# Selective scans of two Mamba blocks: B products of three channel blocks through ScalarE and TensorE, C products of three on GpSimd

## The reference, cut to what matters

```python
delta = softplus(dt @ Wdt.T + dt_bias)
def step(state, xs):
    d_t, B_t, C_t, u_t = xs
    dA = jnp.exp(d_t[..., None] * A)
    state = dA * state + (d_t * u_t)[..., None] * B_t[:, None, :]
    y_t = jnp.einsum('bdn,bn->bd', state, C_t)
    return (state, y_t)
y = ys + u * D_param
y = y * silu(gate)          # layer 1 only
```

## Time and profile before

| what | before |
|---|---|
| time, median of 3 runs | 3902.34 us (3901.07 to 3902.68) |
| the profiled execution's own time | 3894.73 us |
| span of that execution in the trace | 3893.0 us |
| first scan stage with its opening | about 1085 to 1306 us |
| second and third, with openings | about 3337 to 3554, and 3555 to 3773 us |
| VectorE busy, whole span | 2307.4 us (59%) |
| ScalarE, GpSimd busy, whole span | 1531.7 us (39%), 1403.3 us (36%) |
| TensorE busy, whole span | 3553.1 us (91%) |
| mean granted TensorE clock | 0.963 |

### The profile page before, as it was taken

One profiled execution on the slowest core, in us unless ns is written; L12 is line 12 of the kernel. 1 busy time (PEld: TensorE's weight loads), 2 busy tenths in 40 slices (PEclk: granted clock), 3 DMA queues, 4 the chain that ended last, 5 costly groups with the idle time before them and its releaser, 6 DMA issues. The chain is left out here.

```text
span 3893.0 us, 74546 instructions
## 1 busy us (share of the span) xinstructions
PE 3553.1 (91%) x32040; PEld 2424.9 (62%) x32040; DVE 2307.4 (59%) x2562; ACT 1531.7 (39%) x2204; POOL 1403.3 (36%) x894
## 2 busy tenths in 40 slices
PE   6999999999768679999999999999999999686888
PEld 4556555555333455788888888888888847333334
DVE  4666666666369952555555555555555426698972
ACT  2555555555267421222222222222222103676740
POOL 3344444442079520122222222222222004597971
PEclk8999999999779889999999999999999999798999
DMA  6445555553122032011111111111111211221220
GB/s 207 127 138 149 139 139 148 142 137 92 39 92 92 20 141 87 25 43 36 49 41 49 41 49 41 47 43 41 49 41 45 78 52 37 80 92 60 92 66 22
DMA packets 229072, 302.22 MB, mean 78 GB/s; under 512 B 68592, under 2 KB 166864, under 8 KB 227456
## 3 DMA queue, kind: packets, MB, share of 16 engines
q1 hardware_dynamic: 228744, 297.45, 25.9%
HBM read 243.80 MB, written 53.13 MB: 76 GB/s over the span
## 5 line engine op out<-in xcount | busy, mean ns | idle before, releaser
L1764 POOL TENSOR_TENSOR D_ctx_lo<-D_ctx_raw,D_ctx_hi 128x2048 fp32r<-128x2048 f32 (+1 forms) x64 | 269.1, 4205 | 1218.6 <-ACT D_ctx_hi L1758 1218.6
L762 DVE TENSOR_REDUCE A_mxc<-A_psX 128x2 f32<-128x768 f32 (+2 forms) x512 | 485.4, 985 | 208.1 <-PE A_psX L792 207.2
L1058 ACT ACTIVATE A_probs<-A_psE 128x1024 f32<-128x1024 f32 (+1 forms) x416 | 426.2, 1025 | 318.0 <-PE A_psE L1091 312.9
L1783 ACT ACTIVATE D_V<-D_psY 128x384 f32<-128x384 f32 x208 | 101.9, 490 | 904.7 <-PE D_psY L1849 904.7
L1799 DVE TENSOR_REDUCE D_mxc<-D_psE 128x4 f32<-128x1536 f32 (+2 forms) x128 | 241.9, 1890 | 234.9 <-PE D_psE L1877 234.9
L2140 ACT ACTIVATE D_probs<-D_psE 128x2048 f32<-128x2048 f32 x112 | 210.5, 1879 | 296.0 <-PE D_psE L2253 296.0
L2269 PE MATMUL D_psO<-D_probs,D_V 128*32 128x256 f32 (+1 forms) x5376 | 313.3, 381 | 0.0
L1839 PE MATMUL D_psY<-D_ctx_hi,D_wk_hi 128*128 128x384 f32 (+2 forms) x768 | 279.8, 364 | 13.6 <-DVE D_K_lo L1794 12.7
L1849 PE MATMUL D_psY<-D_wv_hi,D_ctx_hi 128*128 128x384 f32 x832 | 285.6, 343 | 0.0
L1849 PE MATMUL D_psY<-D_wv_hi,D_ctx_lo 128*128 128x384 f32 x832 | 279.0, 335 | 0.0
L1849 PE MATMUL D_psY<-D_wv_lo,D_ctx_hi 128*128 128x384 f32 x832 | 278.7, 335 | 0.0
(11 more groups left out here) (376 smaller groups left out, 7797.5 us busy)
## 6 DMA issues: line engine op xcount, KB each, us to landing
A_land<-in_ctx SPq DMA_DIRECT2D x32, 768.0 KB, 6.0
D_ctx_raw<-in_ctx SPq DMA_DIRECT2D x32, 768.0 KB, 4.6
A_land<-in_ctx SPq DMA_DIRECT2D x16, 1024.0 KB, 5.7
D_ctx_raw<-in_ctx SPq DMA_DIRECT2D x16, 1024.0 KB, 5.3
E_Bn<-bc_scratch SPq DMA_DIRECT2D x64, 256.0 KB, 3.6
E_Cn<-bc_scratch SPq DMA_DIRECT2D x64, 256.0 KB, 3.4
k_scratch<-A_Khl SPq DMA_DIRECT2D x32, 384.0 KB, 5.4
A_Kst<-k_scratch SPq DMA_DIRECT2D x64, 192.0 KB, 3.6
```

Of the source, the lines that this page charges most:

```text
L762: nc.vector.tensor_reduce(mxc[:, u % 4, :, u // 4], psX[:, x % 2, :, 0:w], axis=AX_X, op=ALU.max).then_inc(x_free, 1)
L1058: nc.scalar.activation(probs[0:KW[k], n % NPR, :, :].rearrange("p h q -> p (h q)"), psE[0:KW[k], :], ACT.Exp, scale=HD ** -0.5).then_inc(e ...
L1764: nc.gpsimd.tensor_tensor(ctx_lo[c][:, :, 0:w], ctx_raw[c][:, :, 0:w], ctx_hi[c][:, :, 0:w].bitcast(F32), ALU.subtract).then_inc(lo_done[c ...
```

## The change

`B_ON_PE` becomes (0, 1, 2), so the entering terms of three blocks come through ScalarE and TensorE, and GpSimd makes only that of c = 3. `c_on_pool` becomes c > 0, so VectorE keeps only the C product of c = 0. The PSUM banks are now acc 4, h 1, dB 3, and all decays go to a ring of three SBUF buffers. The states that GpSimd reads (h_sb) are written over the part of du that is no longer needed; a row `B_du<-BS_dA,BS_dB` in the order below is such a scan. Rings change: dBx 4 to 2, hc 4 to 2, h_sb and hcp 3 to 4.

The openings change in three ways: the last du product is on VectorE instead of GpSimd, a one-column Exp is issued behind the Ln's, and the scan stage starts after four scaled copies instead of eight.

```diff
-B_ON_PE = (0, 2)
+B_ON_PE = (0, 1, 2)
 def c_on_pool(half, n, c):
-    return c in (1, 3) or c == 2 and n % 2 == 1
+    return c > 0
...
-        NS, NH, NP = 4, 4, 3
+        NS, NH, NP, ND, NE = 2, 2, 4, 3, 3
...
-        dA = r.ps("dA", [P, NA, HALF])
-        dA_sb = r.sb("dA_sb", [P, 2, HALF])
+        dA = r.sb("dA", [P, ND, HALF])
         h = r.ps("h", [P, HALF])
-        dB = r.ps("dB", [P, NB, HALF])
-        h_sb = r.sb("h_sb", [P, NP, HALF])
+        dB = r.ps("dB", [P, NE, HALF])
+        h_sb = du[:, 0:2, :].rearrange("p c (n t) -> p (c n) t", n=NP // 2)
...
         def decay(s):
-            return dA_sb[:, nth_pe[s] % 2, :] if s in nth_pe else dA[:, nth_b[s] % NA, :]
+            return dA[:, s % ND, :]
         def summed_at(s):
-            return s + (2 if s in nth_dve else 3)
+            return s + (2 if s in nth_dve else 4)
         def finished_at(s):
-            return s + (4 if STEPS[s][2] in B_ON_PE else 6)
+            return s + (4 if s in nth_dve else 7)
...
-                for m, i in pieces[:2 * TILES]:
+                for m, i in pieces[:TILES]:
                     times_b(m, i)
...
-                    if decay_ago(s) is not None:
-                        act.wait_ge(h_ready, decay_ago(s) + 1)
+                    if s >= ND:
+                        act.wait_ge(h_ready, s - ND + 1)
...
-                    for m, i in pieces[ahead:ahead + 1]:
+                    for m, i in pieces[ahead:ahead + (2 if s < TILES else 1)]:
...
-                multiplied = 0
-                for k, s in enumerate(b_on_pool):
-                    if k >= NS:
-                        while on_pool[multiplied] <= b_on_pool[k - NS]:
-                            times_c(on_pool[multiplied])
-                            multiplied += 1
+                for s in b_on_pool[:NS]:
                     times_b(s)
-                    half, n, c = STEPS[s]
-                    if gate is not None and half and n in (3, 6, 9, 12) and c == 1:
+                for s, (half, n, c) in enumerate(STEPS):
+                    if s in nth_pool:
+                        times_c(s)
+                    if s in nth_b and nth_b[s] + NS < len(b_on_pool):
+                        times_b(b_on_pool[nth_b[s] + NS])
+                    if gate is not None and half and n in (3, 6, 9, 12) and c == CN - 1:
                         gated_output(CN * (N_STATE - 1) + n // 3 - 1)
...
-                nc.vector.memset(dA[:, :, :], 0.0).then_inc(cleared, 1)
-                nc.vector.memset(dA_sb[:, :, :], 0.0).then_inc(cleared, 1)
+                nc.vector.memset(dA[:, :, :].rearrange("p k (b t) -> p k b t", t=S)[:, :, :, 0], 0.0
+                                 ).then_inc(cleared, 1)
...
-                for s in range(len(STEPS) + 3):
-                    if s in nth_pe and nth_pe[s] + NB < len(b_on_pe):
-                        entering(nth_pe[s] + NB)
+                for s in range(len(STEPS) + 4):
+                    if s in nth_pe and nth_pe[s] + NE < len(b_on_pe):
+                        entering(nth_pe[s] + NE)
...
-                        if c in B_ON_PE:
+                        if c in B_ON_PE or k == CN - 1:
                             dve.wait_ge(delta_made, k + 1)
                             nc.vector.tensor_tensor(du[:, c, :], delta[:, c, :], XnT[:, c, :], ALU.mult
                                                     ).then_inc(du_made, 1)
...
-                    for k, c in enumerate(ORDER):
+                    for k, c in enumerate(ORDER[:CN - 1]):
                         if c not in B_ON_PE:
                             pool.wait_ge(delta_made, k + 1)
...
+                    nc.scalar.activation(early[:, :], bias[:, 0:1], ACT.Exp)
```

More of the change, by code:

```diff
@@ L318, in _ @@
                 ahead = 0
-                for m, i in pieces[:2 * TILES]:
+                for m, i in pieces[:TILES]:
                     times_b(m, i)
                     ahead += 1
-                act.wait_ge(cleared, 2)
+                act.wait_ge(cleared, 1)
                 for s, (half, n, c) in enumerate(STEPS):
-                    if decay_ago(s) is not None:
-                        act.wait_ge(h_ready, decay_ago(s) + 1)
+                    if s >= ND:
+                        act.wait_ge(h_ready, s - ND + 1)
                     nc.scalar.activation(decay(s).rearrange("p (b t) -> p b t", t=S)[:, :, 1:S],
@@ L358, in times_c @@
                                             ALU.mult).then_inc(hcp_ready, 1)
-                multiplied = 0
-                for k, s in enumerate(b_on_pool):
-                    if k >= NS:
-                        while on_pool[multiplied] <= b_on_pool[k - NS]:
-                            times_c(on_pool[multiplied])
-                            multiplied += 1
-                    times_b(s)
-                    half, n, c = STEPS[s]
-                    if gate is not None and half and n in (3, 6, 9, 12) and c == 1:
+                for s in b_on_pool[:NS]:
+                    times_b(s)
+                for s, (half, n, c) in enumerate(STEPS):
[4 more added lines that the diff above has]
+                    if gate is not None and half and n in (3, 6, 9, 12) and c == CN - 1:
                         gated_output(CN * (N_STATE - 1) + n // 3 - 1)
-                for s in on_pool[multiplied:]:
-                    times_c(s)
             @block.vector
             def _(dve):
-                nc.vector.memset(dA[:, :, :], 0.0).then_inc(cleared, 1)
-                nc.vector.memset(dA_sb[:, :, :], 0.0).then_inc(cleared, 1)
+                nc.vector.memset(dA[:, :, :].rearrange("p k (b t) -> p k b t", t=S)[:, :, :, 0], 0.0
+                                 ).then_inc(cleared, 1)
                 def scan(s):
@@ L381, in scan @@
                         dve.wait_ge(db_full, nth_pe[s] + 1)
-                        entering = dB[:, nth_pe[s] % NB, :]
+                        entering = dB[:, nth_pe[s] % NE, :]
                     else:
@@ L435, in entering @@
                     pe.wait_ge(scaled_ready, TILES * (m + 1))
-                    if k >= NB:
-                        pe.wait_ge(h_ready, b_on_pe[k - NB] + 1)
+                    if k >= NE:
+                        pe.wait_ge(h_ready, b_on_pe[k - NE] + 1)
                     for i in range(TILES):
-                        last = nc.tensor.transpose(dB[:, k % NB, bass.ts(i, P)], scaled[:, m % 3, i, bass.ts(j, P)],
+                        last = nc.tensor.transpose(dB[:, k % NE, bass.ts(i, P)], scaled[:, m % 3, i, bass.ts(j, P)],
                                                    consts["ident"][:, :])
                     last.then_inc(db_full, 1)
-                for k in range(NB):
+                for k in range(NE):
                     entering(k)
@@ L1216, in l0_mamba @@
             q = Region(nc, inner, "B1")
+            early = q.sb("early", [P, 1])
             ps = q.ps("ps", [P, 8, 512])
@@ L2364, in l1_mamba @@
         ws = r.sb("ws", [P, DI], F32R)
-        duT = r.sb("duT", [P, NPAIR, len(B_ON_PE) * P])
         pr = r.sb("pr", [P, NPAIR, RN])
@@ L2376, in l1_mamba @@
             up = q.sb("up", [P, 2, B, PADDED])
-            eu = duT[:, :, :].rearrange("p t n -> p (t n)").rearrange("p (n t) -> p n t", n=2)
+            eu = q.sb("eu", [P, 2, TOK])
             wdt = q.sb("wdt", [P, DI])
@@ L2618, in l1_mamba @@
             q.restart()
+        duT = r.sb("duT", [P, NPAIR, len(B_ON_PE) * P])
         out_done = r.sem("out_done")
@@ L2684, in _ @@
                                 nc.scalar.activation(du[:, c, :], du[:, c, :], ACT.Ln, bias=1.0).then_inc(ln_made, 1)
+                            nc.scalar.activation(early[:, :], cols[:, 0, 0:1], ACT.Exp)
                             for k, c in enumerate(B_ON_PE):
@@ L2692, in _ @@
                         def _(pool):
-                            for k, c in enumerate(ORDER):
+                            for k, c in enumerate(ORDER[:CG - 1]):
                                 if c not in B_ON_PE:
@@ L2713, in _ @@
                                                         ).then_inc(delta_made, 1)
-                                if c in B_ON_PE:
+                                if c in B_ON_PE or k == CG - 1:
                                     dve.wait_ge(delta_made, k + 1)
```

5 lines of the change are left out of this document (removed).

## The result

| what | before | after |
|---|---|---|
| median of the comparison on one chip | 3901.70 us (8 runs, 3892.96 to 3906.52) | 3911.45 us (8 runs, 3906.68 to 3916.33) |
| ratio to before, 95% interval | | 1.0027 (1.0016 to 1.0038) |
| the profiled execution's own time | 3894.73 us | 3910.63 us |
| span of that execution | 3893.0 us | 3908.9 us |
| VectorE, ScalarE, GpSimd busy, whole span | 2307.4, 1531.7, 1403.3 us | 2342.1, 1576.8, 1413.3 us |

The change makes the kernel slower, by 6 to 15 us. VectorE has 48 C products fewer, and yet it is busy 35 us longer. That is where to look.

What follows compares the result with a forecast made beforehand. VectorE (5.58 us a state) bounded it narrowly over GpSimd (5.54); after the change, GpSimd (5.89). Stages +5, +6, +6 and openings -3.6 gave +13, taken as +14: 3916 us, range 3842 to 3938.

Steps and rivals of the forecast that it cites:

- The steady state without contention: Scan stages: VectorE's four scans and one C product make 5.08 us a state, 0.50 less than before.
- the first rival: Scan stages: scans don't take turns, 5.08 us a state, 56 us less, 3846 us; chance 0.16.
- The turns: Scan of c = 3, two SBUF inputs: alternates with GpSimd's instructions, costing GpSimd 0.97 us a state, period 5.89; chance 0.67.
- the sign: Scan stages: whether the change is slower or faster, said to turn at about 0.5 us of GpSimd's time a state.
- the second rival: Scan of c = 3: turns cost GpSimd only 0.4 to 0.8 us a state, 3859 to 3898 us; chance 0.11.
- GpSimd's next product: Scan stages, a rival: it goes before the waiting scan, 6.5 us a state, 3974 us; chance 0.06.
- The slow clock: TensorE at a stage's start: sums and entering terms late by a few us; inside the range, no chance given.
- The openings: Before each of three scan stages: 1.2 us less, as GpSimd makes no du product; -3.6 us in all.
- The start of a stage: First scan 3.3 us after the stage's start instead of about 5.4, first C product at 5.8 instead of 7.8.
- The stage counted on GpSimd: Start, products, turns and early waits sum to 192.8 us in the first stage, 197.7 in the other two.
- The end of the third stage: VectorE's finishes and gate products behind GpSimd's last product: about 2.2 us left instead of 4.7, -2.5.
- An addition 0.43: TensorE in the scan stages: an addition takes 0.43 us, so transposes and sums make 3.1 us a state.

Runs made afterwards that it cites:

- the last experiment: Changed kernel with c = 3 decay in PSUM and two dB banks, but old openings (fourth du product on GpSimd, no early Exp): 3855.42 us, ratio 0.9886.

## Why the prediction was right

**Direction and size.** Forecast 3916 us and slower; measured 3911.45, slower by 0.27% with all of the interval above zero. The three stages grew by 14.1 us in the trace, forecast 13.

**The steady state without contention, 5.08 us.** Right: 5.10 with the decay in PSUM. That kernel, in which no scan takes turns, ran at 3847.93 us; the first rival's sum for a kernel without turns was 3846.

**The turns.** This was the step that decided the sign, and it rested on two places of the trace in other instructions. A scan waits as they do. Forecast 0.97 of GpSimd's time a state, measured 5.845 - 4 x 1.23 = 0.93; period 5.89 against 5.84 to 5.85. The end of the scan, forecast 1.05 us behind GpSimd's, was 1.09 behind it.

The rule of the Trainium skill (SBUF — State Buffer, "Who interferes with whom"), that a VectorE instruction with two SBUF inputs and a GpSimd instruction that reads SBUF exclude each other, names no scan. The trace agrees with it for `tensor_tensor_scan` too: 1.99 us in SBUF, 1.20 with the decay in PSUM.

**How near the sign was.** The prediction has the sign turn at about 0.5 us of GpSimd's time a state. By its own sum that is wrong: +14 us over 96 states is 0.15 a state, so it turns at 0.97 - 0.15 = 0.82, and the second rival's 0.8 gives 3898, already faster. With 0.93 measured, "slower" was right by 0.11 us a state, a narrower margin than the 0.4 to 0.5 that the prediction's figure suggests.

**The other rivals.** A price of 0.4 to 0.8 was too low. GpSimd's next product never went before a waiting scan: no scan of dA and dBx in the three stages lasts over 2.27 us, where 3.3 would have shown it. The slow clock did no visible harm: of the full 2.4 GHz, TensorE was granted 0.50 from 1120 to 1125, 0.81 to 1130 and 1.00 behind that (before, 0.50 until 1130), and GpSimd's first C product came as forecast.

**Which engine bounds.** Right: GpSimd has no idle time in the steady state, and VectorE's 0.8 us of room lie inside the scan. I had forecast a mean of 2.1 for that scan; it is 1.88 in the first stage.

**The openings, -1.2 each.** They gave -0.9, -1.3 and -2.0, together -4.2 against the forecast -3.6. The first lost 0.44 to a turn with GpSimd's CW_d_lo, which overlaps it here and not in the profiled execution of before. The early Exp at no cost: right, at 1111.42 ScalarE would have waited anyway.

**The start of a stage.** First scan at 3.41 (forecast 3.3), first C product at 5.82 (5.8). A table load took 1.28 us wherever it stood (1118.20, with the next instruction at 1119.50, in the last experiment), and without it the first scan of before came 1.2 us sooner. The Trainium skill (ScalarE: Activation LUTs, "What ACT_TABLE_LOAD costs") adds 1.38 us of draining to it, by which it would have been more than 2.5; no row shows that.

**The stage counted on GpSimd.** 192.25 (forecast 192.8) and 197.25 (197.7). Two small errors partly cancel in the first: 32 turns of 0.93 would be 30 us instead of 31, which leaves about 1.7 us of waits instead of 1. The end of the third stage became shorter by 1.4 and not by 2.5: VectorE's last gate product ended at 3788.70, and the second of the four took 1.44 us instead of 0.69, with a turn inside. This term was off by about half.

**What was wrong without doing harm.** "An addition 0.43" and "3.1 us a state" on TensorE: it is 0.86 and 4.8. At 5.84 a state it stayed hidden, but the step by which I ruled TensorE out left it 2.8 us of room, and there was 1.0. For the version with 5.10 it would have misled.

## What to carry to other kernels

Where VectorE and GpSimd both work on SBUF, price each VectorE instruction with two SBUF inputs twice: once on VectorE, and once on GpSimd as its own length less 0.1 to 0.3 us. That is what the scan and the product cost here, with fp32 tiles of 128x512 and GpSimd full. Put one input in PSUM for the long ones first. The kernel in which only the scan had two SBUF inputs ran at 3911 us, the one in which only the product had them at 3884, and the one with neither, whose bank came from a ring of three, at 3848. When both engines show 100% busy, compare the durations of one form of instruction across the stage: the shortest and the median, 1.19 and 1.99 here, tell how much of "busy" is waiting.

## What the runs showed that I had not expected

- A short hold between two engines can cost more than itself, through the queue of a third. With h in SBUF the hold on GpSimd was only 0.45 to 0.57 us, yet the state grew by 0.86, through VectorE's scan, TensorE's queue and a ring of four buffers. In such a kernel a price in one engine's time is a lower bound, and the length of each loop of waits has to be added up too.
- The same instructions in the same order can run at two periods, 5.96 and 5.37 us, in the two halves of one stage.
- Here an fp32 matmul of 512 columns comes as two instructions of 0.43 us, while four transposes of 128 columns come as four with 0.46 together. So before a row's time is multiplied, its count in the trace has to be compared with the count in the program.
